# A four-layer graph network on one core: one-hots of targets stored in the second pass and read back in later ones

## The reference

```python
h = relu(layernorm(x));  x = x + L0(h, ...)   # per edge: row of (source, type of 16), times a weight, summed by target
h = relu(layernorm(x));  x = x + L1(h, ...)   # Chebyshev, K = 3: prop(h), then prop(prop(h)), products with W, relu
h = relu(layernorm(x));  x = x + L2(h, ...)   # attention over edges of 86 types
h = relu(layernorm(x));  x = x + L3(h, ...)   # mean of the sources' rows by target

def prop(v):                                   # in L1
    return segment_sum(w_hat[:, None] * v[src], dst, num_segments=n)
```

## Time and profile before

| | |
|---|---|
| runs of the kernel before, us | 7771.03, 7773.39, 7800.02 (median 7773.39) |
| profiled execution, us | 7774.41, its span 7772.6 |
| busy: PE, DVE, ACT, POOL | 63%, 63%, 30%, 67% |
| mean granted TensorE clock | 0.64 of 2.4 GHz |
| stages on the span, us | pass 0 and what lies before it: to 2300; pass 1: 2328 to 3404; pass 2: 3466 to 4800; attention: 4820 to 6940; pass 4: 7030 to 7727 |

### The profile page before, as it was taken

The page is one execution under the profiler, slowest core; times in us unless marked ns, Lnnn a source line. Parts: engine busy times, 40 slices in busy tenths (PEclk is TensorE's granted clock), DMA queues, the critical chain, the costliest instruction groups (busy, mean ns, idle before and its releaser), DMA issues.

```text
span 7772.6 us, 149728 instructions
## 1 busy us (share of the span) xinstructions
PE 4872.0 (63%) x41375; PEld 4126.7 (53%) x41376; DVE 4897.8 (63%) x16081; ACT 2357.4 (30%) x7420; POOL 5242.6 (67%) x5417
## 2 busy tenths in 40 slices
PE   5333333333337667677777776777777777786777
PEld 2222222222225555566666665677777776775666
DVE  5555555567778888866666665444444444449997
ACT  4444444430012222223544445211121212123322
POOL 2777777777747777757665662677777777756663
PEclk6555555555556776767776776555555555558998
DMA  7111111110012222224656666222222222214443
GB/s 171 14 14 14 14 14 14 14 14 13 13 22 53 52 52 52 52 44 143 213 190 203 201 198 205 59 41 41 41 41 41 41 41 41 41 34 94 100 100 79
DMA packets 464811, 547.95 MB, mean 70 GB/s; under 512 B 217753, under 2 KB 373945, under 8 KB 464629
## 3 DMA queue, kind: packets, MB, share of 16 engines
q0 software_dynamic: 173168, 146.14, 12.7%
q1 hardware_dynamic: 235013, 186.26, 9.4%
q10 hardware_dynamic: 56448, 213.62, 7.0%
HBM read 298.88 MB, written 246.72 MB: 70 GB/s over the span
## 4 chain that ended last, share of the span: by engine, by line
POOL 33%; DVE 21%; issue 18%; PE 17%; DVEq 8%; DMA 2%; ACT 1%; POOLq 0%; ACTq 0%; SPq 0%
POOL arena L712 33%; DVE tbuf L1813 6%; PE ps_agg L1112 6%; DVE tbuf L1806 3%; PE ps_agg L1239 2%; DVEq L1858 2%; DVEq L1561 2%; PE ps_wide L1223 1%; DVE msg L1857 1%; DVE H L1813 1%; DVE msg L1860 1%; PE ps_wide L1342 1%; PE ps_wide L1226 1%; DMA arena<-table,ibuf 1%; DVEq L1863 1%
## 5 line engine op out<-in xcount | busy, mean ns | idle before, releaser
L712 POOL DMA_INDIRECT arena<-table,ibuf x3328 | 3151.3, 947 | 1242.4 <-issue 1129.9
L712 POOL DMA_INDIRECT arena<-nodes,ibuf x2080 | 2088.6, 1004 | 1142.9 <-issue 616.2
L1112 PE MATMUL ps_agg<-mem_b,arena 128*32 128x80 f32 (+1 forms) x3744 | 457.6, 301 | 504.0 <-DVEq L1561 497.7
L1112 PE MATMUL ps_agg<-mem_a,arena 128*32 128x80 f32 (+1 forms) x3744 | 433.0, 291 | 533.0 <-DVEq L1561 511.0
L1112 PEld LDWEIGHTS ps_agg<-mem_b,arena 128*32 128x32 f32 (+1 forms) x3744 | 400.1, 152 | 554.1 <-DVEq L1561 520.9
L1112 PEld LDWEIGHTS ps_agg<-mem_a,arena 128*32 128x32 f32 (+1 forms) x3744 | 378.9, 146 | 592.6 <-DVEq L1561 528.9
L1813 DVE TENSOR_SCALAR tbuf<-iota,at_f 128x256 bf16<-128x256 bf16 x3185 | 680.9, 297 | 0.3 <-PE ps_t L1239 0.3
L1377 PE MATMUL ps_agg<-tbuf,msg 128*64 128x80 f32 x2496 | 373.6, 344 | 337.9 <-DVE msg L2039 337.9
L983 ACT ACTIVATE att<-score 128x8 f32<-128x8 f32 x208 | 43.3, 208 | 1649.1 <-DVE score L2030 1649.1
L1377 PEld LDWEIGHTS ps_agg<-tbuf,msg 128*64 128x64 f32 x2496 | 336.0, 227 | 359.0 <-DVE msg L2039 359.0
L835 ACT ACTIVATE tbuf<-O,tbuf 128x49 bf16<-128x49 bf16 x1664 | 448.5, 363 | 78.3 <-DVE H L1728 78.3
(11 more groups left out here) (388 smaller groups left out, 11745.8 us busy)
## 6 DMA issues: line engine op xcount, KB each, us to landing
table<-tbuf ACTq DMA_DIRECT2D x294, 544.5 KB
idx_a<-lows_d SPq DMA_DIRECT2D x637, 192.0 KB
arena<-table,ibuf POOLq DMA_INDIRECT x3328, 2.4
table<-tbuf ACTq DMA_DIRECT2D x98, 495.0 KB
arena<-nodes,ibuf POOLq DMA_INDIRECT x2080
table<-tbuf SPq DMA_DIRECT2D x25, 1024.0 KB, 4.3
idx_a<-lows_d SPq DMA_DIRECT2D x91, 224.0 KB
nodes<-O SPq DMA_DIRECT2D x7, 224.0 KB, 3.0
```

The source lines that it names most:

```text
L712: nc.gpsimd.indirect_dma_start(out=INTO[s][:, k, c, 0:WIDTH[s]], out_offset=None, in_=TABLE[s], in_offset=bass.IndirectOffsetOnAxis(ap=ibu ...
L1112: last = nc.tensor.matmul(ps_agg[ROW0[s]:ROW0[s] + CHN[s], 0:WIN], narrow[:, k, c, 0:CHN[s]], onehots[b][:, c, :], start=(c == 0), stop=(c ...
```

## The change

In pass 1 each batch's one-hots of targets, once made, are also written to DRAM (`targets_d`, 26 x 128 rows of 49 x 256 bf16) by SyncE. In pass 2 no targets are compared: SyncE reads them back, batch by batch, into the two places of `to_oh`. In pass 4 a turn of three blocks no longer takes blocks 3i, 3i+1, 3i+2 but i, i+13, i+26 (`block_of`); the first of these is among the 26 stored ones and is read back (`RETURNED`), the other two are compared as before; and `to_oh` has four places there, in `O`. VectorE waits in pass 1 for a place's store before it writes it again (`s_kept`); TensorE waits for `s_there` before it sends. In passes 1 and 2 a group is added one step later (steps 3, 5, 7 and 1 of the next block), ahead of the weighing in that step; `add_block` stands behind the split in both; steps that don't weigh a group end in a drain. The gathers' semaphores are shared by passes 1, 2 and 4. The diff, cut:

```diff
+KEPT = BLOCKS[1]
+TO_RING = {1: 2, 2: 2, 4: 4}
+RETURNED = (0,)
+    targets_d = scratch("targets_d", (KEPT * P, NBK * W2), BF16)
-        to_oh = {s: [...] for s in BLOCKS}
+        to_oh = {s: [...] for s in (1, 2)}
+        to_oh[4] = [O[:, at:at + n].bitcast(BF16)... for at, n in ((0, 896), (896, 768), (1664, 768), (2432, 768))]
+        def block_of(s, n):
+            turn, e = divmod(n, UNIT[s])
+            return e * TURNS[s] + turn
...
+            def spread_low(h, i, e, q):
+                s, (b0, n) = (1, 2, 4)[h], BATCHES[q]
+                sp.wait_ge(s_from, ((BEFORE[h] + e) * NBATCH + q + 1) + i * (UNIT[s] * NBATCH))
+                sp.dma_start(lows[q % RING]..., lows_d[...].partition_broadcast(P)).then_inc(s_bc[q % RING], 16)
+            def keep_targets(i, f, q):
+                sp.wait_ge(s_made, (f * NBATCH + q + 1) + i * NBATCH)
+                sp.dma_start(kept_rows(i, f, q), to_oh[1][q % 2]...).then_inc(s_kept[q % 2], 16)
+            def return_targets(h, i, e, q):
+                s = (1, 2, 4)[h]
+                sp.wait_ge(s_sent, ((BEFORE[h] + e) * NBATCH + q + 3 - TO_RING[s]) + i * (UNIT[s] * NBATCH))
+                sp.dma_start(to_oh[s][q % TO_RING[s]]..., kept_rows(i, block_of(s, e), q)).then_inc(s_there[q % TO_RING[s]], 16)
+            def spread_and_keep():
+                late = 6
+                ...
+            def spread_and_return(h, ahead, soon, returned):
+                ...
+                def turn(i, f, last):
+                    for m in range(n):
+                        if m + ahead < n or not last:
+                            spread(i, f, m + ahead)
+                        if m + soon < n or not last:
+                            give_back(i, f, m + soon)
...
-            spread_lows(0)
+            spread_and_keep()
             store_nodes(1, 1, lambda i: ubuf[1][i])
-            spread_lows(1)
+            for j in range(2):
+                sp.wait_ge(s_kept[j], 16 * (KEPT * NBATCH // 2))
+            spread_and_return(1, 5, 0, (0,))
...
-            spread_lows(2)
+            spread_and_return(2, 4, 2, RETURNED)
...
+                    if s == 2:
+                        pe.wait_ge(s_there[q % 2], ...)
+                        carry_wait(pe)
                     if s == 4:
-                        pe.wait_ge(s_to, ...)
+                        pe.wait_ge(s_there[q % 4], ...)
                         carry_wait(pe)
...
                 def compare_targets(i, e, q):
-                    dve.wait_ge(s_sent, count(i, e, q, 1))
+                    dve.wait_ge(s_sent, count(i, e, q, 3 - TO_RING[s]))
+                    if s == 1 and (e > 0 or q > 1):
+                        dve.wait_ge(s_kept[q % 2], 16 * ((e * NBATCH + q) // 2) + i * (16 * NBATCH // 2))
+                        carry_wait(dve)
...
-                        if s == 2 and q % NBATCH == 2 and (q >= NBATCH or not first):
-                            add_block(i, f + q // NBATCH - 1)
...
-                        if goes(q - 1):
+                        if s == 1 and goes(q - 1):
                             compare_targets(i, f, q - 1)
...
+                        if q % NBATCH == 2 and (q >= NBATCH or not first):
+                            add_block(i, f + q // NBATCH - 1)
+                        if q - 3 in HIDDEN[s]:
+                            add_group(s, i, HIDDEN[s][q - 3], f)
+                        if q == 1 and not first:
+                            add_group(s, i, SLOTS - 1, f - 1)
                         if q - 1 in HIDDEN[s]:
                             weigh_group(s, i, HIDDEN[s][q - 1], f=f)
-                        if q - 2 in HIDDEN[s]:
-                            add_group(s, i, HIDDEN[s][q - 2], f)
-                        if q == 0 and not first:
-                            add_group(s, i, SLOTS - 1, f - 1)
-                        if s == 1 and q % NBATCH == 2 and (q >= NBATCH or not first):
-                            add_block(i, f + q // NBATCH - 1)
+                        else:
+                            dve.drain()
...
-                            compare_targets(i, n, q).then_inc(s_to, 1)
+                            if e not in RETURNED:
+                                compare_targets(i, n, q)
```

More of the change, by code:

```diff
@@ L59 @@
 TURNS = {s: n // UNIT[s] for s, n in BLOCKS.items()}
+KEPT = BLOCKS[1]
+TO_RING = {1: 2, 2: 2, 4: 4}
+RETURNED = (0,)
+assert BLOCKS[2] == KEPT and TURNS[4] * len(RETURNED) <= KEPT
 BEFORE = [0, BLOCKS[1], BLOCKS[1] + BLOCKS[2]]
@@ L403, in gnn_kernel @@
         s_got = sem("slots_rows_picked")
-        s_to = sem("targets_compared")
+        s_made = sem("targets_onehots_made")
+        s_kept = [sem(f"targets_onehots_kept_{j}") for j in range(2)]
+        s_there = [sem(f"targets_onehots_there_{j}") for j in range(4)]
         s_wgh = sem("slots_rows_weighed")
@@ L430, in gnn_kernel @@
         for s in range(5):
-            sums[s]["gathered"] = sums[1]["gathered"] if s == 4 else [sem(f"sum{s}_gathered_{k}") for k in range(SLOTS)]
-        GOT = [0, 0, 0, 0, GROUPS[1] // SLOTS * (16 * CH)]
+            sums[s]["gathered"] = sums[1]["gathered"] if s in (2, 4) else [sem(f"sum{s}_gathered_{k}") for k in range(SLOTS)]
+        GOT = [0, 0, GROUPS[1] // SLOTS * (16 * CH), 0, (GROUPS[1] + GROUPS[2]) // SLOTS * (16 * CH)]
         TURNED = [0, NB, None, 2 * NB, 3 * NB]
@@ new lines, in spread_and_keep, with block @@
+            def spread_and_keep():
+                late = 6
+                def block(i, f, first=False):
+                    for q in range(NBATCH):
+                        spread_low(0, i, f, q)
+                        if q >= late:
+                            keep_targets(i, f, q - late)
+                        elif not first:
+                            keep_targets(i, f - 1, q - late + NBATCH)
+                block(0, 0, True)
+                with sp.Fori(0, KEPT - 1) as i:
+                    block(i, 1)
+                for q in range(NBATCH - late, NBATCH):
+                    keep_targets(0, KEPT - 1, q)
@@ new lines, in spread_and_return, with spread, give_back @@
+            def spread_and_return(h, ahead, soon, returned):
+                s = (1, 2, 4)[h]
+                n = UNIT[s] * NBATCH
+                def spread(i, f, m):
+                    spread_low(h, i, (f + m // n) * UNIT[s] + m % n // NBATCH, m % NBATCH)
+                def give_back(i, f, m):
+                    if m % n // NBATCH in returned:
+                        return_targets(h, i, (f + m // n) * UNIT[s] + m % n // NBATCH, m % NBATCH)
+                def turn(i, f, last):
[4 more added lines that the diff above has]
+                            give_back(i, f, m + soon)
+                for m in range(ahead):
+                    spread(0, 0, m)
+                for m in range(soon):
+                    give_back(0, 0, m)
+                with sp.Fori(0, TURNS[s] - 1) as i:
+                    turn(i, 0, False)
+                turn(0, TURNS[s] - 1, True)
@@ L935, in pick_and_lay_out @@
                 if TURNS[s] * SLOTS < GROUPS[s]:
-                    with act.Fori(TURNS[s], GROUPS[s] // SLOTS) as i:
+                    for i in range(TURNS[s], GROUPS[s] // SLOTS):
                         for k in range(SLOTS):
@@ L1860, in pick_weighed @@
                             V.tensor_tensor(rows, of, by.unsqueeze(2).to_broadcast([P, n, D]), ALU.mult).then_inc(s_wgh, 1)
-                        if goes(q - 1):
+                        if s == 1 and goes(q - 1):
                             compare_targets(i, f, q - 1)
                         dve.drain()
-                        if q == 0 and not first:
+                        if s == 1 and q == 0 and not first:
                             start_block(i, f)
@@ L1923, in pick_and_sum @@
                 if s == 1:
+                    for j in range(2):
+                        dve.wait_ge(s_kept[j], 16 * (KEPT * NBATCH // 2))
                     dve.wait_ge(s_own, 1)
```

39 lines of the change are left out of this document (23 added, 16 removed).

## The result

The changed kernel took 7690.4 us (median of 4 runs, 7683.6 to 7693.5) beside 7784.7 us for the kernel before in the same session: a ratio of 0.9882, with a 95% interval of 0.9868 to 0.9896. It is faster by 1.2%, outside the 0.5% that a measurement tells from no change. Against the profiled execution of before, the span went from 7772.6 to 7687.0 us: 85.6 us saved, where I had forecast 219 (7774 to 7555).

What follows compares the result with a forecast made beforehand. GpSimd was taken to bound the second pass, VectorE the last; in the third no engine was full, with TensorE and VectorE handing work back and forth. 7774 - 187 - 40 + 8 = 7555 us, range 7450 to 7695.

Steps and rivals of the forecast that it cites:

- Third pass: Third pass: a block falls from 51.2 to 44.0 us, saving 187 us over 26 blocks.
- the 35.5 that I had left it: Third pass: VectorE's us a block after losing 9.6 of comparisons and most of 6.1 of waiting for group sums.
- From these I estimate 3.3 us for 384 KB alone and 5 to 6 under load: hidden.: Third pass: landing time of a fetch, from landings of 224 KB and 1024 KB and the longest table write, 6.6 us.
- I take 44.0, nearer to GpSimd: Third pass: block time chosen between GpSimd's 41.1 us and 47 us, TensorE's 37.6 plus 9 of remaining waits.
- Last pass: Last pass: a turn's first block falls from 17.5 to 14.4 us, TensorE and transfers limiting; 40 us saved over 13.
- Second pass: Second pass: stores, waits and drains add 0.3 us a block, 8 us over 26, as GpSimd holds the pace.
- B: Rival: TensorE and hand-overs hold the third pass at 48 us; last pass 20, second -20; total 7691; chance 0.17.
- A: Rival: TensorE's clock rises; third pass at GpSimd's 41.1 us saves 263, last pass 48; total 7463; chance 0.18.
- C: Rival: comparisons filled VectorE's waiting anyway; third pass 50 us (31 saved), last 0, second -20; total 7763; chance 0.06.
- the rule on gathers: Third pass: VectorE's two-port modes block GpSimd's descriptor writing; fewer comparisons give a floor near 40 us instead of 41.1.
- D: Rival, all three block passes: 384 KB transfers land late, slower from 10 us landing; 7994 at 11 us; chance 0.04.
- The adds: Third pass: adding a group's sum two steps after its weighing removes most of VectorE's 6.1 us a block of waiting.

Runs made afterwards that it cites:

- four places: Changed kernel with 24 drains ahead of the last pass and four places instead of two for split slot rows in the third pass: ratio 0.9743.
- changed kernel with drains: Changed kernel with 24 drains put once into VectorE's program ahead of the last pass, nothing else moved: ratio 0.9814.
- four places and small returns: Changed kernel with 24 drains, four places for split slot rows in the third pass, and returns of one slot of six or seven: ratio 0.9684.
- small returns: Changed kernel with returns of one slot of six or seven after the first third-pass block and first last-pass turn; wrong sums: ratio 0.9813.

## Why the prediction was wrong, step by step

**Third pass: mis-sized.** The forecast was 44.0 us a block, the measurement 47.1. VectorE did drop out (it was 608.38 us busy in the 1140 from 3560, or 25.1 us a block, and the 35.5 that I had left it held its other waits too), and the wait for the group's sum has left the list, both as I had said. Two steps failed.
- "From these I estimate 3.3 us for 384 KB alone and 5 to 6 under load: hidden." No wait of TensorE for a return stands in the list of the third pass (3560 to 4700), so the fetch itself was hidden, but its load was not: with a sixth of the bytes a block was 1.6 us shorter. I had written that transfers would be 90% busy (86.7% measured, 40.8 us of a block where I had 39.5) and that they would queue, and then cost that at nothing. Which transfer was late in whose path I did not find.
- "I take 44.0, nearer to GpSimd, since the largest waits in the list ... both stand behind work that goes." The wait of TensorE for the comparison of sources did not go. Before it was (3560 to 4700; after: 134.1, above):

```profile
PE ps_wide L1223 <- DVE H L1806: 148.6, 50, 3.7
```

  The comparison is queued on VectorE behind the rest of the split, which waits for ScalarE, which waits for TensorE's sums two batches back. That ring was in part covered by comparisons of targets (two more places are worth 1.0 us with them and 2.0 without). TensorE's wait for the comparison stays even with four places (157.3 us of its weight loads), so the ring does not explain all of it. With both causes taken away the block is 43.7 us. So 44.0 was a fair figure for what GpSimd and TensorE allow, and the 3.4 us in between are the gap.

**Last pass: the mechanism right, and something missing from the sum.** I had the first block at 14.4 us and 40 us for the pass. In the changed kernel it was 15.2 us and the pass lost 4. With the loop moved the first block is 14.1 us and the pass 50 us shorter than before (675.7 to 625.8). The block by TensorE and by transfers, 13.8 to 14.2 us, was well sized; the extra gain is in the block before it, 17.2 to 16.5 us, for which I have no cause shown. What failed is that no step asked where VectorE's loop would stand. "Sorting, attention and the norms have no edit in their loops: 0" was true, but an edit ahead of a loop moves the loop. It cost the changed kernel 53 us by the two ratios, 54 by the two passes.

**Second pass: right.** I took 0.3 us a block. The profiles of the first session give 41.4 against 40.8 us, but across chips before itself moves: 41.16 us on the chip where the changed kernel with drains had 41.37. So it is 0.2 us a block, and VectorE's list of waits in the second pass has none for a store. The later adds take another 0.4 us off what would be there without them. The third pass began 12 us later than before in the profiled executions, of which chips and stores each hold a part.

**The sum again, from measurements.** By spans: +12 in front of the third pass, -101 in it, +4 in the last pass, and the rest under 1, is -86. Forecast: +8, -187, -40. Of the 133 us between them, 54 are code fetches and 3.1 x 26 = 81 us are the third pass's ring and load. What is left nearly cancels: the last pass without the fetches gains 10 us more than forecast, the third pass begins 12 us later instead of 8, and I had counted 26 blocks where 25 intervals are measured.

**The rivals.** B (TensorE and the hand-overs hold the third pass at 48 us, total 7691) came out within 1 us of the measured time, partly by luck: its third pass is right in kind and within 0.9 us, its last pass had 20 us of gain and there was none, for a reason it did not name, and its second pass had 20 us of loss where there were 12. A did not come: the clock rose only from 0.73 to 0.79 in the third pass (0.85 at best, with four places and small returns). In attention it stayed at 0.50. C, which had 31 us for the third pass, was refuted by its 101. The floor near 40 us that I took from the rule on gathers did not come either: a gather took 819.11/844 = 0.97 us in the third pass after 0.98 before, with VectorE 52% busy after 68%. The second pass spoke against it already, with 0.98 at 85%. For D, TensorE waited for returned one-hots only in the last pass, 0.8 us at most in the ten turns.

**The adds.** I gave 6.1 us a block of VectorE's waits to adding a group's sum later. The wait did go, but with the adds early again and no fetch stall the pass was only 0.2 us a block slower: VectorE is 25 us busy and has 47 to do it in, and even with 241.0 us of this wait the pass loses nothing more. It was worth next to nothing.

## What to carry to other kernels

Any edit in an engine's program moves all loops behind it. When a stage that was not edited changes, or a jump costs an engine a few us of "issue", look first at the count of instruction fetches in that stage; then move the loop by some instructions and time that before you judge the edit itself. When an engine's work is taken away, follow the ring of hand-overs that it had covered, with its places two batches back: the gain stops there and not at the next engine's busy time. A transfer that lands in time can still cost by its load, here with the queues 87% busy.

## What the hardware did that I had not expected

- VectorE's loop of 336 instructions (328 compiled) was fetched anew in each turn from one place and not from another 24 instructions on: 48 fetches of 8 KB against 4 in ten turns, and 53 us of 7690.
- The same stall cost 1.8 us a turn with the queues 40% busy (the kernel before moved, the block at the jump from 17.2 to 19.0 us) and 4.1 us with the queues 58% busy in the changed kernel (16.5 to 20.7), whose turns also bring returns. With small returns it was 2.6 us, so the returns' load makes it longer; by which path I did not find. Some of the fetches in the changed kernel took 1.2 to 1.5 us, most 0.3 to 0.6. In the third pass with the early adds it cost 8.2 us a block.
